# Output bias on GpSimd, gates only where they are used, ranks a pass earlier, token chunks first: a GNN with a mixture of experts on one core

## The reference

```python
x = x + gnn(layernorm(x))          # 1250 nodes, 512 features, 40000 edges and 1250 loops
x = x + ffn(layernorm(x))          # mixture of 8 experts on T = 512 tokens
```

```python
h = relu(A @ (h0 @ W1.T) + b1)     # A = diag(dinv) Adj diag(dinv), 512 -> 128
z = A @ (h @ W2.T) + b2            # 128 -> 64
y = relu(z @ Wd1.T + bd1)          # 64 -> 128
y = relu(y @ Wd2.T + bd2)          # 128 -> 256
return y @ Wd3.T + bd3             # 256 -> 512, bd3 is the output bias
```

```python
h = gelu(xg @ w1[e])               # 512 -> 256, xg: the tokens of expert e
y = h @ w2[e]                      # 256 -> 512
out[token] += weight * y
```

## Time and profile before

| | |
|---|---|
| median of 3 runs | 192.22 us (191.41 to 193.18) |
| the profiled execution | 192.37 us, of which the span of the trace is 190.6 us |
| TensorE busy | 165.4 us (87%) |
| VectorE busy | 130.9 us (69%) |
| ScalarE busy | 93.0 us (49%) |
| GpSimd busy | 96.2 us (50%) |
| mean granted clock of TensorE | 0.959 of full speed |
| shares of the chain of waits | TensorE 57%, VectorE 15%, GpSimd 9%, DMA 6% |

### The profile page before, as it was taken

How to read it: one execution, slowest core, us unless ns; L and a number is a source line. 1 busy time by engine, 2 the same in 40 slices (tenths; PEclk the granted TensorE clock), 3 DMA queues, 4 the chain that set the end, 5 groups by cost and what they waited for, 6 DMA issues and landing times.

```text
span 190.6 us, 3626 instructions
## 1 busy us (share of the span) xinstructions
PE 165.4 (87%) x1179; PEld 115.6 (61%) x1179; DVE 130.9 (69%) x304; ACT 93.0 (49%) x202; POOL 96.2 (50%) x74
## 2 busy tenths in 40 slices
PE   4599799999997999479999999779999999999900
PEld 1288578887884665166554454249877777687500
DVE  2898999999995999937031859562697669664210
ACT  3437677777877530034045127021986777644310
POOL 5099999999990000000007000686008888763662
PEclk9999999999999999979999999985999999999995
DMA  4994000000004899980000005247915366543564
GB/s 123 299 331 126 2 2 3 3 0 3 3 0 88 274 380 367 365 293 10 0 0 3 0 0 220 69 132 252 379 54 70 79 127 82 101 48 51 72 80 64
DMA packets 15547, 21.71 MB, mean 114 GB/s; under 512 B 3135, under 2 KB 8001, under 8 KB 15525
## 3 DMA queue, kind: packets, MB, share of 16 engines
q1 hardware_dynamic: 12994, 16.02, 25.6%
q0 software_dynamic: 2432, 5.24, 15.7%
q10 hardware_dynamic: 98, 0.17, 0.2%
HBM read 15.19 MB, written 6.23 MB: 112 GB/s over the span
## 4 chain that ended last, share of the span: by engine, by line
PE 57%; DVE 15%; POOL 9%; DMA 6%; issue 6%; ACT 4%; POOLq 1%; ACTq 0%; DVEq 0%
PE bank L1428 9%; PE bank L1670 8%; PE bank L1531 7%; PE bank L1697 5%; PE bank L1403 4%; PE bank L1641 4%; PE bank L1681 4%; PE bank L1700 3%; DVE x_sb L896 3%; DVE ring L705 3%; PE bank L1682 3%; DMA out<-at,to_i 3%; POOL first_viol L598 2%; POOL out L647 2%; DMA x_rows<-at 2%
## 5 line engine op out<-in xcount | busy, mean ns | idle before, releaser
L616 POOL TENSOR_SCALAR_AFFINE_SELECT before<-ones_bf 128x128 bf16<-128x128 bf16 x1 | 37.8, 37836 | 0.0
L647 POOL DMA_INDIRECT out<-at,to_i x16 | 23.9, 1494 | 20.9 <-DVE at L1063 10.1
L1428 PE MATMUL bank<-ring 128*128 128x110 bf16 x324 | 29.9, 228 | 5.2 <-DVE ring L705 3.7
L1531 PE MATMUL bank<-at,ring 128*128 128x512 bf16 (+1 forms) x150 | 29.1, 353 | 0.5 <-ACT ring L1197 0.5
L1428 PEld LDWEIGHTS bank<-ring 128*128 128x128 bf16 x324 | 20.5, 101 | 12.0 <-issue 5.1
L705 DVE TENSOR_TENSOR ring<-iota_slots,lo 128x1024 bf16<-128x1024 f16 (+1 forms) x41 | 27.4, 667 | 0.0
L1156 ACT CAST at<-bank 128x400 f32 (+1 forms) x41 | 20.6, 503 | 10.9 <-PE bank L1434 8.7
L705 DVE TENSOR_TENSOR ring<-iota_dst,key 128x880 bf16<-128x880 f16 (+1 forms) x41 | 24.3, 594 | 0.0
L1531 PEld LDWEIGHTS bank<-at,ring 128*128 128x128 bf16 x150 | 14.9, 101 | 13.2 <-issue 1.1
L1670 PE MATMUL bank<-at_r 128*128 128x512 f32 (+1 forms) x64 | 21.8, 404 | 0.0
L1003 DVE TENSOR_TENSOR ew_r<-ew,at_r 128x1024 fp32r<-128x1024 f32 x16 | 19.3, 1216 | 0.0
(11 more groups left out here) (208 smaller groups left out, 297.0 us busy)
## 6 DMA issues: line engine op xcount, KB each, us to landing
ew<-in_w SPq DMA_DIRECT2D x16, 512.0 KB, 9.6
x_sb<-in_x SPq DMA_DIRECT2D x9, 256.0 KB, 5.4
out<-x_sb SPq DMA_DIRECT2D x9, 256.0 KB
...
```

The source lines that it names most:

```text
L616: nc.gpsimd.affine_select(out=before[:, :], in_=ones_bf[:, :], compare_op=ALU.is_gt, fill=0.0, base=0, pattern=[[1, P]], channel_multiplie ...
L647: nc.gpsimd.indirect_dma_start(out, bass.IndirectOffsetOnAxis(to_i[0:n, i, e:e + 1].bitcast(mybir.dt.uint32), 0), y_out[0:n, e % 2, i], No ...
L1428: last = mm(to, hot_src[:, j, t], hot_dst[:, j, t], start=(t == 0 and not ends), stop=(first and t == tiles - 1), skip_group_check=not ends)
L1531: last = mm(bank[4 + i][:, 0:n], parts[k][:, s], at[:, s, a:a + n], start=(k == 0 and s == 0), stop=(k == last_k and s == CH - 1))
```

## The change

- **Bias.** The ten additions of `bd3` to `x_sb` move from VectorE to GpSimd, into its queue behind the constants, ahead of the memset that waits for the first convolution. They wait for the small weights (`s_wg`, whose last part is b2) and for VectorE's last reading of `x_sb` (`s_deg_var`). Each signals `s_xb`, and VectorE's additions in the decoder wait for it.
- **Gates.** The dense gates are computed in the dense path alone.
- **Ranks.** `rank_assignments` moves from behind pass two to behind `spread_dinv`, that is between pass one and two.
- **Decoder.** `decode3` of the four token chunks comes first, then `decode1(2)`, `decode2(1)`, `decode2(2)`, then the other six chunks. `decode2(2)` gets banks 2 and 3. The transposes of a token of the dense path wait for `s_y2` in place of `s_y1`.
- **Normalising.** VectorE takes tokens 0, 1 and 3, ScalarE token 2; ScalarE takes the square root before `finish_y2(1)` and token 2 behind it. Then ScalarE runs one gelu on a spare value, which loads its table there.
- **Experts.** VectorE's second weight split comes between chunks 7 and 8 and not behind the last; the wait for all ten `s_x2` moves from ahead of the first transposes to ahead of `down_slots(0)`; `keep_results(e - 1)` moves ahead of the rest of the hidden values of e; `y_out` has three buffers (KEPT = 3), of which the third lies in the same matrix memory, and a buffer's next writer waits for the scatter-adds of three experts before.

```diff
@@ -225,7 +225,8 @@
...
         x2_more = at2_flat[:, 3 * NP:3 * NP + 2 * D].rearrange("p (b n) -> p b n", b=2)
-        y_out = at2_flat[:, 0:4 * D].rearrange("p (b h n) -> p b h n", b=2, h=2)
+        KEPT = 3
+        y_out = [at2_flat[:, o:o + 2 * D].rearrange("p (h n) -> p h n", h=2) for o in (0, 2 * D, 8 * D)]
         rank_hot = ring[:, 5 * NP:5 * NP + J * SLOTS].rearrange("p (j n) -> p j n", j=J)
@@ -431,9 +434,12 @@
...
         WARM = 9
+        DVE_TOKENS = (0, 1, 3)
+        ACT_TOKENS = 2
         SECOND_ROOTS = 4
...
         D1_BANK = [3, 2, 3]
+        D2_BANKS = [(0, 1), (0, 1), (2, 3)]
@@ -541,8 +547,9 @@
...
                 for i, rows in enumerate((xn, x2_more)):
-                    sp.wait_ge(s_xn2, i + 1)
-                    sp.wait_ge(s_xn2_odd, i + 1)
+                    sp.wait_ge(s_xn2, i + 2)
+                    if i == 1:
+                        sp.wait_ge(s_xn2_act, 1)
                     sp.dma_start(x2_rows[2 * i * P:2 * (i + 1) * P, :].rearrange("(c p) n -> p c n", p=P),
@@ -617,6 +624,11 @@
...
+            pool.wait_ge(s_wg, 16 * NWG)
+            pool.wait_ge(s_deg_var, 1)
+            for c in range(CH):
+                nc.gpsimd.tensor_tensor(x_sb[:, c], x_sb[:, c], bd3_sb[:, :], ALU.add).then_inc(s_xb, 1)
+
             pool.wait_ge(s_agg1, len(SPANS))
@@ -646,7 +658,7 @@
...
                                                      bass.IndirectOffsetOnAxis(to_i[0:n, i, e:e + 1].bitcast(mybir.dt.uint32), 0),
-                                                     y_out[0:n, e % 2, i], None, compute_op=ALU.add
+                                                     y_out[e % KEPT][0:n, i], None, compute_op=ALU.add
                                                      ).then_inc(s_added[e % 2], 16)
@@ -891,17 +903,6 @@
...
-            dve.wait_ge(s_wg, 16 * NWG)
-            for c in range(CH):
-                last = v.tensor_tensor(x_sb[:, c], x_sb[:, c], bd3_sb[:, :], ALU.add)
-            link(last)
-            for c in range(TC):
-                for k in range(TOPK):
-                    last = v.tensor_scalar(gate_part[:, k, c], expert_no[:, :], gif[:, c, k:k + 1], gw_sb[:, c, k:k + 1],
-                                           ALU.is_equal, ALU.mult)
-            link(last)
-            link(v.tensor_tensor(gate[:, :, :], gate_part[:, 0], gate_part[:, 1], ALU.add))
-
             routed = [0]
@@ -1016,6 +1017,7 @@
...
             for c in range(CH):
+                dve.wait_ge(s_xb, c + 1)
                 dve.wait_ge(s_d3, c + 1)
@@ -1030,12 +1032,13 @@
...
                         dve.wait_ge(s_rstd2, 1)
-                        for t in range(1, TC, 2):
+                        for t in DVE_TOKENS:
                             v.tensor_scalar(normal(t), x_sb[:, t], rstd[:, 0, t:t + 1], rstd[:, 1, t:t + 1], ALU.mult,
-                                            ALU.add).then_inc(s_xn2_odd, 1)
+                                            ALU.add).then_inc(s_xn2, 1)
                 if c == TC + 1:
                     weights_rest(0)
-            weights_rest(1)
+                if c == TC + 3:
+                    weights_rest(1)
             with dve.If(sparse != 0):
@@ -1058,9 +1061,9 @@
...
                     dve.wait_ge(s_down_sp, 2 * e + 1)
-                    if e >= 2:
-                        dve.wait_ge(s_added[e % 2], 32 * (e // 2))
-                    v.tensor_scalar(y_out[:, e % 2, 0], bank[4 + 2 * (e % 2)][:, 0:D], slot_weight[:, 0, e:e + 1], None,
+                    if e >= KEPT:
+                        dve.wait_ge(s_added[(e - KEPT) % 2], 32 * ((e - KEPT) // 2 + 1))
+                    v.tensor_scalar(y_out[e % KEPT][:, 0], bank[4 + 2 * (e % 2)][:, 0:D], slot_weight[:, 0, e:e + 1], None,
                                     ALU.mult).then_inc(s_y, 1)
@@ -1071,10 +1074,10 @@
...
                         second_parts(e + 2, W_HI + 1, 0)
+                    if e >= 1:
+                        keep_results(e - 1)
                     dve.wait_ge(s_hs_hi, e + 1)
                     v.tensor_tensor(hs[:, e % 2, 1], hs_raw, hs[:, e % 2, 0].bitcast(F32), ALU.subtract).then_inc(s_hs_lo, 1)
-                    if e >= 1:
-                        keep_results(e - 1)
                     if e + 2 < NE:
@@ -1082,6 +1085,14 @@
...
             with dve.If(dense != 0):
+                for c in range(TC):
+                    for k in range(TOPK):
+                        last = v.tensor_scalar(gate_part[:, k, c], expert_no[:, :], gif[:, c, k:k + 1], gw_sb[:, c, k:k + 1],
+                                               ALU.is_equal, ALU.mult)
+                last.then_inc(s_gate, 1)
+                dve.wait_ge(s_gate, 1)
+                v.tensor_tensor(gate[:, :, :], gate_part[:, 0], gate_part[:, 1], ALU.add).then_inc(s_gate, 1)
+                dve.wait_ge(s_gate, 2)
                 for c in range(TC):
@@ -1243,11 +1254,12 @@
...
                     act.wait_ge(s_d2, 2 * i + k + 1)
-                    nc.scalar.activation(y2t[:, k, a:a + n], bank[k][:, 0:n], ACT.Relu, bias=bd2_sb[:, k:k + 1]).then_inc(s_y2, 1)
+                    nc.scalar.activation(y2t[:, k, a:a + n], bank[D2_BANKS[i][k]][:, 0:n], ACT.Relu,
+                                     bias=bd2_sb[:, k:k + 1]).then_inc(s_y2, 1)
...
                 nc.scalar.activation(normal(c), x_sb[:, c], ACT.Identity, scale=rstd[:, 0, c:c + 1],
-                                     bias=rstd[:, 1, c:c + 1]).then_inc(s_xn2, 1)
+                                     bias=rstd[:, 1, c:c + 1]).then_inc(s_xn2_act, 1)
@@ -1262,14 +1274,14 @@
...
             finish_y1(2)
-            finish_y2(1)
...
             nc.scalar.activation(rstd[:, 1, 0:TC], mv[:, 0:TC, 1], ACT.Sqrt, bias=eps[:, :]).then_inc(s_std2, 1)
+            finish_y2(1)
             act.wait_ge(s_rstd2, 1)
-            for c in range(0, TC, 2):
-                normalise_tokens(c)
+            normalise_tokens(ACT_TOKENS)
             finish_y2(2)
+            nc.scalar.activation(table_use[:, :], one[:, :], ACT.Gelu)
             with act.If(sparse != 0):
@@ -1588,6 +1598,11 @@
...
+            def spread_and_rank():
+
+                spread_dinv()
+                rank_assignments()
+
             def rows_of_slots():
@@ -1599,7 +1614,7 @@
...
             neighbours([part[:, 0], part[:, 1], part[:, 2]], wait_part1, s_agg1,
-                       lambda i: product_h2(0) if i == 1 else None, spread_dinv, rank_assignments)
+                       lambda i: product_h2(0) if i == 1 else None, spread_and_rank)
             product_h2(1)
@@ -1627,9 +1642,10 @@
...
                 for k in range(2):
-                    if i >= 1:
-                        pe.wait_ge(s_y2, 2 * (i - 1) + k + 1)
-                    mm(bank[k][:, 0:n], wd2t_sb[:, k * P:(k + 1) * P], y1t[:, a:a + n], start=True, stop=True).then_inc(s_d2, 1)
+                    if i == 1:
+                        pe.wait_ge(s_y2, k + 1)
+                    mm(bank[D2_BANKS[i][k]][:, 0:n], wd2t_sb[:, k * P:(k + 1) * P], y1t[:, a:a + n], start=True,
+                       stop=True).then_inc(s_d2, 1)
@@ -1654,14 +1673,13 @@
...
             decode1(1)
-            for c in range(CH):
-                if c == TC - 1:
-                    decode2(1)
+            for c in range(TC):
                 decode3(c)
-                if c == 0:
-                    decode1(2)
-                if c == TC:
-                    decode2(2)
+            decode1(2)
+            decode2(1)
+            decode2(2)
+            for c in range(TC, CH):
+                decode3(c)
@@ -1710,7 +1728,6 @@
...
-                pe.wait_ge(s_x2, CH)
                 transpose_gathered(0)
@@ -1719,6 +1736,8 @@
...
                         transpose_gathered(e + 2)
+                    if e == 0:
+                        pe.wait_ge(s_x2, CH)
                     down_slots(e)
```

21 lines of the change are left out of this document (12 added, 9 removed).

## The result

The changed kernel took **195.65 us** (median of 4, 194.68 to 196.64) against 192.0 us before: a ratio of 1.018, 95% interval 1.011 to 1.026. It is slower (the whole interval lies above 1), where 182.1 us was predicted. A second set of runs on another chip (e17) gave 195.39 us and 1.012 (1.006 to 1.018). The profiled execution took 195.35 us, with a span of 193.6 us and a granted clock of 0.943.

A forecast was written before the change was run, and what follows sets the result against it. It took VectorE's chain of waits ahead of the W2 product, low clock behind TensorE's idle stretches and the scatter-add tail as bounds: 192.37 - 3.77 - 1.2 + 1.2 - 4.95 - 1.4 = 182.25, less 0.15: 182.1 us, range 179.8 to 190.0.

The forecast's parts named there:

- So GpSimd loses against an unbroken row of VectorE work and gets in at its breaks: Bias additions before the ranks: GpSimd delays VectorE only at breaks between linked instructions; basis of the 1.2 us loss.
- I take two additions ahead of s_chosen: Before the ranks: two GpSimd additions of 1.0 us delay VectorE, less 0.84 slack, a loss of 1.2 us.
- The third rival: GpSimd gets an addition into each of six breaks before s_chosen, one before: 188.8 us (chance 0.14), or 195.8 (0.07).
- The stall of 3.77 and 1.2 us of clock: At the product by W2: TensorE's 3.77 us wait goes whole, and the clock no longer falls behind it, 1.2 us.
- Decoder and transposes, 4.95 us: End of decoder: token chunks first, transposes not behind the last chunk; `down_slots(0)` starts 4.95 us earlier, 2.45 of it clock.
- I take the clock as staying at 2.4 GHz: At the first experts: TensorE's idle time falls to some 0.3 us, so the clock holds, worth 2.45 us.
- the first rival: The clock falls again at the start of the experts, 2.45 us come back: 184.6 us, chance 0.12.
- Tail, 1.4 us: End of kernel: results scaled before the next expert's remaining hidden values, so the chain of scatter-adds comes 1.4 us earlier.
- The third buffer at nothing: Expert results: the third result buffer was priced at no gain, as the last scatter-adds wait for expert 6's anyway.
- The scatter-adds as the bound: Rival: late landing of output stores holds result 0 and the scatter-add chain, 184.9 us, chance 0.10.
- it doesn't do what it says: Rival: another wait holds the W2 product, so 3.77 and 1.2 us stay: 187.1 us, chance 0.07.

The follow-up runs named there:

- e17: The changed kernel itself, run again on the chip of e15: 195.39 us, ratio 1.012 to the kernel before.
- e2: The changed kernel with the ten bias additions back on VectorE, where it waits (seven behind the slot arithmetic, one behind each scaled sum): 190.17 us.
- e4: The kernel before with only decoder, transposes and results changed; bias, gates and ranks as before: 189.94 us, ratio 0.988.
- e12: The kernel of e10 with results as in the kernel before (two buffers, later scaling): 185.21 us.
- e15: The kernel of e2 run again on a fourth chip: 184.71 us, ratio 0.958 to the kernel before.
- e6: The changed kernel with GpSimd adding a constant in place of the bias row, so one SBUF input instead of two: 189.45 us.
- e18: The kernel of e14 run again on the chip of e15: 184.60 us, ratio 0.959 to the kernel before.
- e9: The kernel of e2 with products of zeros among the transposes of experts 0 and 1, output stores held until both first up products are done: 185.47 us.
- e10: The kernel of e2 with the output stores held until both first up products are done: 184.22 us.
- e11: The kernel of e2 with products of zeros among the transposes of experts 0 and 1, and results as in the kernel before: 186.42 us.
- e14: The kernel of e2 with results as in the kernel before (two buffers, later scaling): 185.00 us.
- e13: The kernel of e2 with the output stores held until the first half of the first up product is done: 185.56 us.

## Why the prediction was wrong

It was 13.5 us too low, and by the ledger (13.1 in the profiled executions): 8.3 at the start of layer 2, 3.3 from there to `down_slots(0)`, 1.5 behind it.

**The step that failed** is "So GpSimd loses against an unbroken row of VectorE work and gets in at its breaks", and with it "I take two additions ahead of s_chosen". It is the other way round: the additions took turns with the unbroken row of two-input instructions, and all ten were done before the linked chain with its breaks began. I had read the rule off a row in which VectorE compared 16-bit one-hots, and carried it over to f32 instructions with two SBUF inputs. Nothing in that row spoke of those. Nor does the rule hold for that row: in e2, e4 and e12 the same affine_select got into it (last section). The third rival had the right mechanism at the wrong place, and too few turns. An addition takes 1.26 to 1.31 us, where I had 1.0, and a turn costs VectorE 1.0 (1.35 less 0.34). Ten turns would make s_chosen 10 us late; it was 8.5 late, since the first additions ran ahead of VectorE's row. The term stood at 1.2 us in the sum; one chip shows 9.0 for it at the start of layer 2 (e17 against e15). The wait is 4.96 us in the changed kernel, 6.53 in e17, where the first sum began 1.2 us sooner: s_chosen comes at 75.7 to 76.1 in all four traces with the additions there.

The Trainium skill, page "SBUF — State Buffer", section "Who interferes with whom", says that a VectorE instruction with two SBUF inputs contends with a GpSimd instruction that reads SBUF. The rows of L869 agree, and I set that sentence behind a row that was not about it. The same section says of VectorE's 2-port modes that who issues first blocks the other for the whole instruction; the prediction put the two together, and the rows of L869 show turns, one for one. e6 bounds it: a GpSimd instruction with one SBUF input cost VectorE a third of that.

**The stall of 3.77 and 1.2 us of clock: right to 0.3 us.** W2 starts without a wait in every kernel with the first half. In e18 layer 2 begins 4.74 us earlier than before (83.11 against 87.85), predicted 4.97. In e15 it is 3.30, because the first sum ran partly at 1.2 GHz (7.04 us for 5.57).

**Decoder and transposes, 4.95 us: the mechanism right, the clock not.** In e15 the stretch from layer 2 to `down_slots(0)` is 4.40 us shorter (45.13 against 49.53); the 0.5 that lack are a wait of 0.83 for the second gather. Its issue took 1.71 us instead of 0.96, because the second pair of weight splits (L1003 in e15, L1004 in the changed kernel), which the change moved ahead of the last chunks, now ran beside it. That reading is argued from timelines, no run took the splits away. In the changed kernel 1.6 us are left, since "I take the clock as staying at 2.4 GHz" failed. Among the nine traces from the last two chips without additions on GpSimd it stayed in five (e9, e10, e11, e14, e15; e9 and e11 with products of zeros) and fell in four; with the first rival's 2.45 us I had the price (7.93 - 5.88 = 2.05 here), but gave it 0.12.

**Tail, 1.4 us: seldom there.** Of 14 traces with the results' change the tail is 7.7 to 7.9 us in three (e9, e13, e15) and 8.7 to 9.7 in the others; without it 9.4 to 10.0. The earlier issue is there: the last scatter-add but two begins 0.9 us ahead of the end of TensorE's last product in the changed kernel and in e15, and 0.8 behind it before. What decides is how long it takes to land, which the last one waits for: GpSimd's timeline of e15 has it 4.05 us ahead of the last one, that of the changed kernel 5.70, before it was 3.75.

```profile
172.67 1.33 POOL L654 DMA_INDIRECT out<-at,to_i  x1 [0.30 <-issue]
174.31 1.56 POOL L654 DMA_INDIRECT out<-at,to_i  x1 [0.30 <-ACT at L1314]
176.72 1.33 POOL L654 DMA_INDIRECT out<-at,to_i  x1 [0.85 <-DMA out<-at,to_i]
```

I counted the earlier issue and took the landing as unchanged; why it is longer in most traces stays open. Medians show nothing of the term in e15 against e18, 1.0 us in e10 against e12. The third buffer at nothing: no run took it alone.

**The scatter-adds as the bound** and **"it doesn't do what it says"** did not come. The version that the runs point to is e15: the whole change with the additions on VectorE where it waits for layer 2. It takes 184.71 us, 4.2% less than before.
